# Waiting for each gather's rows before the next gather is issued, in a four-layer graph attention kernel

## What is computed

```python
def _L0_gnn_ref(inputs, adj, W, a):
    Wh = inputs @ W                                            # 4096 x 64
    e = (Wh @ a_src)[:, None] + (Wh @ a_dst)[None, :]          # 4096 x 4096
    e = jnp.where(e > 0, e, ALPHA * e)
    scores = jnp.where(adj > 0, e, NEG_BIG)
    attention = jax.nn.softmax(scores, axis=1)
    return jax.nn.elu(attention @ Wh)
x = _layernorm(x + _L0_gnn_ref(x, adj, W0, a0))
# layers 1, 2 and 3 in the same way on the new x; layer 1 adds a bias and has no elu
```

## Time and profile before

| | |
|---|---|
| timed executions | 600.36, 600.63, 600.85 us, median 600.63 |
| profiled execution, its own span | 859.9 us |
| TensorE busy in the profiled execution | 419.1 us (49%) |
| ScalarE busy | 400.8 us (47%) |
| VectorE busy | 349.6 us (41%) |
| GpSimd busy | 278.0 us (32%), 292 gathers |
| DMA | 84.86 MB, mean 99 GB/s |
| mean granted TensorE clock | 0.815 |

### The profile page before, as it was taken

How to read it: one execution, slowest core, us unless ns; L and a number is a source line. 1 busy time by engine, 2 the same in 40 slices (tenths; PEclk the granted TensorE clock), 3 DMA queues, 4 the chain that set the end, 5 groups by cost and what they waited for, 6 DMA issues and landing times.

```text
span 859.9 us, 10681 instructions
## 1 busy us (share of the span) xinstructions
PE 419.1 (49%) x3453; PEld 334.5 (39%) x3453; DVE 349.6 (41%) x1601; ACT 400.8 (47%) x876; POOL 278.0 (32%) x296
## 2 busy tenths in 40 slices
PE   2354512246655786411129983310499633104985
PEld 1243301245543675300119862210397522004964
DVE  3035813744379598200003872300048622000587
ACT  2677612555476476200325971231269612313684
POOL 0000173140320410777710034777100437771000
PEclk9999999999999998555559995755599857555997
DMA  8999962482673100222200012222000112220000
GB/s 312 428 330 428 422 198 58 173 290 100 212 282 124 17 26 27 32 27 27 27 8 2 20 30 29 28 27 27 9 1 20 34 26 27 28 28 6 8 19 28
DMA packets 20546, 84.86 MB, mean 99 GB/s; under 512 B 6083, under 2 KB 11462, under 8 KB 16262
## 3 DMA queue, kind: packets, MB, share of 16 engines
q1 hardware_dynamic: 10102, 73.15, 21.8%
q0 software_dynamic: 9344, 9.89, 9.4%
q10 hardware_dynamic: 1040, 1.08, 0.4%
HBM read 78.72 MB, written 5.37 MB: 98 GB/s over the span
## 4 chain that ended last, share of the span: by engine, by line
another core or an unknown queue 23%; PE 17%; DVE 12%; ACT 11%; issue 9%; DVEq 0%; ACTq 0%
PE bank L709 7%; ACT arena L865 4%; PE bank L689 3%; PE bank L672 3%; ACT arena L851 2%; DVE x L1313 2%; PE bank L670 1%; DVE stats L1295 1%; PE bank L705 1%; ACT arena L875 1%; DVE arena L1232 1%; ACT arena L839 1%; PE bank L574 1%; DVE res L1292 1%
## 5 line engine op out<-in xcount | busy, mean ns | idle before, releaser
L528 POOL DMA_INDIRECT xg<-table,index x292 | 277.8, 951 | 499.4 <-DMA table<-wh 299.8
L1232 DVE CUSTOM_DVE_ANT_0 arena<-bank,arena 128x256 f32<-128x256 f32 (+3 forms) x123 | 63.4, 523 | 284.7 <-ACT arena L851 224.5
L851 ACT ACTIVATE arena<-bank,sloped_own 128x256 f32<-128x256 f32 (+3 forms) x123 | 68.5, 557 | 176.3 <-remote 109.7
L689 PE MATMUL bank<-packed,arena 128*128 128x128 f32 x339 | 68.3, 323 | 120.0 <-issue 74.0
L839 ACT ACTIVATE arena<-arena,half 128x4096 bf16<-128x4096 int32 x31 | 114.7, 3703 | 19.1 <-DMA arena<-in_adj_t 18.5
L689 PEld LDWEIGHTS bank<-packed,arena 128*128 128x128 f32 x339 | 46.0, 165 | 132.7 <-issue 118.5
L875 ACT COPY arena<-bank 128x256 f32<-128x256 f32 (+3 forms) x123 | 54.1, 446 | 75.4 <-remote 55.4
L670 PE MATMUL bank<-off_row,wall 128*128 128x256 bf16 (+3 forms) x132 | 43.9, 332 | 81.2 <-issue 58.4
L709 PE MATMUL bank<-xg,arena 128*128 128x64 f32 x486 | 73.0, 284 | 10.6 <-ACT arena L875 8.6
L709 PEld LDWEIGHTS bank<-xg,arena 128*128 128x128 f32 x486 | 63.7, 197 | 24.0 <-ACT arena L875 13.5
L1029 DVE MAX8 top<-bank 128x8 f32<-128x256 f32 x31 | 13.4, 431 | 131.5 <-remote 69.5
(11 more groups left out here) (148 smaller groups left out, 780.1 us busy)
## 6 DMA issues: line engine op xcount, KB each, us to landing
arena<-in_adj_t SPq DMA_DIRECT2D x31, 2048.0 KB
xg<-table,index POOLq DMA_INDIRECT x292
table<-wh SPq DMA_DIRECT2D x24, 132.0 KB, 1.7
arena<-in_adj SPq DMA_DIRECT2D x1, 2048.0 KB, 12.9
table<-wh ACTq DMA_DIRECT2D x1, 1056.0 KB
x<-in_x SPq DMA_DIRECT2D x1, 1024.0 KB, 15.0
out_x<-x SPq DMA_DIRECT2D x8, 128.0 KB, 1.9
packed<-in_c_packed SPq DMA_DIRECT2D x1, 312.0 KB
```

The costliest lines, as they stand in the source:

```text
L528: pool.indirect_dma_start(out=xg[:, c, :], out_offset=None, in_=table[l][0:rows, :], in_offset=bass.IndirectOffsetOnAxis(ap=index[:, c:c + ...
L689: t = nc.tensor.transpose(turned_ps[turned_bank(n)][:, c * P:(c + 1) * P], scores(l, n)[:, c * P:(c + 1) * P], ident[:, :])
L851: nc.scalar.activation(scores(l, n)[:, 0:m * P], score_ps[n % len(score_ps)][:, 0:m * P], ACT.Relu, bias=sloped_own[:, k:k + 1], scale=ALP ...
L1232: nc.vector.tensor_tensor_reduce(out=y, in0=score_ps[n % len(score_ps)][:, 0:m * P], in1=y, scale=-1.0, scalar=-FLOOR, op0=ALU.add, op1=AL ...
```

## The change

`gather` keeps a list of what it has issued. Before each gather but the first, GpSimd now waits until the gather issued last has landed: all 16 of its increments on the semaphore of its tile. The order of the gathers, their buffers and their number stay as they are; in a layer's first gather the wait is for the last gather of the layer before.

```diff
         @block.gpsimd
         def _(pool):
+            sent = [0] * TILES
+            in_flight = []
+
             def gather(l, k, c, rows=N):
 
+                if in_flight:
+                    pool.wait_ge(*in_flight[-1])
                 pool.indirect_dma_start(
                     out=xg[:, c, :], out_offset=None, in_=table[l][0:rows, :],
                     in_offset=bass.IndirectOffsetOnAxis(ap=index[:, c:c + 1], axis=0),
                 ).then_inc(gathered[k], 16)
+                sent[k] += 1
+                in_flight.append((gathered[k], 16 * sent[k]))
```

## The result

The change makes the kernel 1.75 times as long. Four executions took 1047.50 to 1052.57 us, median 1050.99, against 600.74 before: ratio 1.7476, 95% interval 1.7433 to 1.7518. The forecast was 900, its range ended at 955: the direction was right, the size was not. The profiled execution's span is 1050.8 us, so here timed and profiled agree.

What follows compares the result with a forecast made beforehand. The prediction took GpSimd's gather stream to pace layers 1 to 3. Layer 1's start at 346, 218 periods of 2.45 us (534), 2.17 last landing, 14.3 to the end and 2 for clock gave 898.5, forecast 900 us, range 838 to 955.

Steps and rivals of the forecast that it cites:

- The price of one round trip: Start to start of gathers on GpSimd: 2.17 us landing plus 0.28 to the next start, 2.45 instead of 1.25.
- The bound of 2.9: Upper bound for a gather's period in us, if landing (2.3), wake-up and 0.30 of issue add.
- rows 7: Profile rows of DMA packets of the gathers issued at 776.68 and 297.82, read as landing after 2.17 and 2.3 us.
- Layer 0: 29 gathers at 4.3 us beside mask loads until 227, 44 in 108 us; layer 1 starts at 346 instead of 309.
- the tail: Behind the last gathers: 2.17 us last landing, 14.3 from last spread to end, 2 for matmuls at a lower clock.
- The timed clock: Times of the 859.9 us profiled execution with late starts and idle taken out, 603.3 us; layer 1 starts near 309.
- The gather stream paces layers 1 to 3: In timed executions of the kernel before, GpSimd's gathers set the pace, at about 93 us a layer.
- A: Rival: layer 0 hides its round trips; total 863 us; chance 0.14.
- B: Rival: round trips are shorter without the profiler, period 2.1 us or less; total 795 us; chance 0.13.
- D: Rival: faster, since with one gather in flight the other engines get through; total 555 us; chance 0.02.
- E: Rival: no change, the wait is already satisfied when GpSimd reaches it; about 600 us; chance 0.02.
- C: Rival: round trips are longer than one quiet row, 2.75 us; total 977 us; chance 0.11.

Runs made afterwards that it cites:

- e3: Changed kernel with eight gathers in flight and a semaphore per chunk: 600.95 us, ratio 1.0000 to the kernel before.
- e12: Changed kernel with a small memset between wait and gather in layers 1 to 3: 1115.71 us, ratio 1.8590 to the kernel before.
- e9: Kernel before, unchanged, profiled a second time: 601.23 us, profiled span 599.4.
- e6: Kernel before without the gathers of layers 1 to 3, computing on stale rows: 587.79 us, ratio 0.9785.
- e7: Kernel before with a small memset, and a wait for it, behind each gather of layers 1 to 3: 630.46 us, ratio 1.0506.
- e11: Changed kernel with each chunk fetching consecutive table rows instead of the tile's neighbours: 982.61 us, ratio 1.6452 to the kernel before.
- e8: Changed kernel with gathers of layers 1 to 3 fetching 64 of their 128 rows: 996.68 us, ratio 1.6588 to the kernel before.

## Why the prediction was right and wrong

**Direction and mechanism: right.** The landing is exposed, once a gather; GpSimd's queue paces all four layers; busy time is unchanged; the waits for indices go; profiled and timed times agree. `e3` and `e12` show the cause from both sides: the same waits cost nothing when the landing is hidden, and work in the loop counts in full when it isn't.

**The price of one round trip: the step that failed.** I had 2.17 to the last packet and 0.28 to the next start, 2.45. The trace has 2.99, beyond the 2.7 that I had named as a sign of being wrong. Two terms were too small:

- From the last packet to the last increment on the semaphore are 0.34 us, which I put at nothing. GpSimd waits for the increment, and packets don't show it. The page of before gave no landing for the gathers, so I read packets in its place and took their end for the landing. The trace of before keeps only 3 of the 16 increments of the gather at 776.68 and the last of them lies 2.69 us behind its start. The bound of 2.9 that I had worked out and set aside was near, but for another reason: its added 0.30 was for issue.
- The last packet ends at 2.36 as a mean, not at 2.17. I took the end from the last digit of the slices, and as the trace of after shows, that digit stands where a last packet begins. The single records of the very two gathers in rows 7 end at 2.36 and 2.44 us, where I had 2.17 and 2.3. So the rows were fair ones, and the reading that I used was wrong by 0.19.

With 0.54 for each of 218 periods that is 118 us in layers 1 to 3. The formula of the Trainium skill (DMA: Bandwidth & Descriptors, Anatomy of one DMA) gives an estimate of 2.08 us for the landing; the trace has 2.70, and the measurement decides. What the prediction took from the same section of the Trainium skill, that most of its 2.0 us is spent waiting for the write to be confirmed, doesn't show here: 1.65 us pass before the first packet and 0.34 behind the last. That my reading came out near the formula made me surer of it than I should have been.

**Layer 0: the shape was right, the size was not.** I had 346 for layer 1's first gather, and it is 381.6. The two rows that decide are GpSimd's 30th gather and TensorE's spread of tile 31:

```profile
237.07 0.95 POOL L533 DMA_INDIRECT xg<-table,index  x1 [1.75 <-DMA xg<-table,index]
```

```profile
370.28 0.39 PE L677 MATMUL bank<-off_row,wall 128*128 128x256 bf16 x1 [0.45 <-DMA xg<-table,index]
```

29 round trips end at 237.1 (I had 227): beside the mask loads, whose last packets begin at 222.3, the first 25 took 5.6 us each and not 4.3, while the first gather started at 84.4 and not at 102.8. The other 44 took 133 us and not 108, by the same 0.6 us each. From the spread to layer 1's first gather are 11.3 us, where I had 10.8. 10 + 25 + 0.5 = 35.5 us. Why the first gather starts near 84 in some executions and near 103 in others stays open; it moves the end little (`e3` starts at 85.1 and has a span of 597.4, `e9` 103.3 and 599.4).

**The sum of the miss.** 118 + 35.6 in layer 0 - 1.7 for the tail (16.8 instead of 18.5) = 152, and 898.5 + 152 = 1050.5, the measured 1050.8 but for rounding.

**The timed clock: right in its total, wrong in its parts.** The late starts were an accident of one execution, as I took them, and the reconstruction of 603.3 was near 599.4. But its parts were off by 18 us in layer 0 and 5 us a layer the other way. They cancelled, and for the forecast neither mattered, as both were replaced by GpSimd's new chain.

**"The gather stream paces layers 1 to 3": wrong, but near.** `e6` and `e7` show compute at 97 to 98 us with gathers 6 us beneath. Had the price of a round trip been below 1.34 us, this would have decided whether the wait costs anything.

**The rivals.** A, B, D and E are refuted: layer 0 paid 90 us, a round trip was longer and not shorter than read, and no gain was seen at any depth. A has a grain of truth, since from layer 0's last gather to layer 1's first there are 36.3 us in `e9` (255.20 to 291.45) and 14.0 after, so 22 us of the delay are hidden there. C came nearest and had 0.11. Of its two arguments the first, that some packets come later than in the quiet row, fits the slow packets; the second, that table writes disturb them, was not tested. Neither contains the 0.34 us to the increment. Its 2.75 us are still 0.24 short of 2.99. The range was too narrow for one reason: it took its spread from cases of overlap, and gave the unit price little, though it was multiplied by 263 and rested on one reading. One tenth of a us of it is 26 us of the total.

## What to carry to other kernels

A transfer's price in a chain runs from its issue to the increment that the waiting engine sees, as a mean over many, not to the last digit of a row of packets; where such a price is multiplied by hundreds, its uncertainty is the range. The depth that hides it is the landing over the issue time: here 2.99 us over 1.25 us, so three in flight are enough and eight bring nothing more. And where a profiled execution is 43% longer than the timed ones, profile again before a single row of it is used.

## What the runs showed of the hardware

- An indirect gather of 128 rows of 264 bytes: first packet 1.65 us behind GpSimd's start, last packet's end 2.36 as a mean, increment 2.70, next gather 2.99. The rows travel in 16 packets of 2112 bytes, most of which take 0.1 to 0.3 us.
- Other rows (`e11`) take away only 0.25 us of this, and half as many rows (`e8`) about as much: 2.74 and 2.73 us a period. The two may be the same 0.25 us.
- Beside 2 MB loads the same gather takes 5.6 us from start to start, as a mean of 25 (84.38 to 224.69).
- TensorE's granted clock was lower where it idled more. The windows of layer 1 in the kernel before (`e9`) and after, one row each (stretch, its length, PE, PEld, DVE, ACT and POOL busy, clock, DMA share, GB/s):

```profile
291.45:389.20 97.75, 74.78 (x511) 61.40 (x514) 46.27 (x223) 62.54 (x183) 69.21 (x73) 0.84 0.23 35
```

```profile
381.60:601.80 220.20, 104.36 (x526) 86.45 (x527) 50.71 (x234) 65.86 (x188) 69.13 (x73) 0.58 0.10 15
```

TensorE is busy 75 of 98 us before and 104 of 220 us after, with waits for rows between its matmuls, and is granted 0.58 in place of 0.84 (1.2 GHz is 0.5, 2.4 GHz is 1); about as many matmuls (526 and 511) keep it busy 104 us instead of 75. Here that costs little, since TensorE has only 2% of the chain that ended last; whether it would be a second price of such a wait in a kernel with less idle time, no run here shows.
